# Two Q/K buffers, even projections, later Q/K copies and bank-by-bank score waits in an attention block

## The reference, cut to what matters

```
h  = layernorm(x);  a = rmsnorm(h) * ln1_w
q, k, v = a @ Wq.T, a @ Wk.T, a @ Wv.T          # 16 heads of 32 columns each
s = q @ k.T / sqrt(32), causal mask             # per head, 512 x 512
p = softmax(s)
mod = 0.1 * tanh((p @ v) @ Wo.T @ A)            # A: 512 x 16
gate = silu(h2 @ W_in.T + (mod * (h2 @ A)) @ B)
out = x + tanh(g) * ((gate * (h2 @ W_up.T)) @ W_down.T)
```

## Time and profile before

| | before |
|---|---|
| median of 3 runs | 1078.74 us (1078.07 to 1079.66) |
| the profiled execution | 1080.39 us, of which the span of the profile 1078.7 us |
| PE busy | 1035.0 us (96%), weight loads 860.9 us (80%) |
| DVE busy | 735.5 us (68%) |
| ACT busy | 613.1 us (57%) |
| POOL busy | 177.7 us (16%) |
| mean granted clock of PE | 0.997 |

### The profile page before, as it was taken

One profiled execution on the slowest core, in us unless ns is written; L12 is line 12 of the kernel. 1 busy time (PEld: TensorE's weight loads), 2 busy tenths in 40 slices (PEclk: granted clock), 3 DMA queues, 4 the chain that ended last, 5 costly groups with the idle time before them and its releaser, 6 DMA issues.

```text
span 1078.7 us, 17949 instructions
## 1 busy us (share of the span) xinstructions
PE 1035.0 (96%) x5336; PEld 860.9 (80%) x5337; DVE 735.5 (68%) x1662; ACT 613.1 (57%) x1463; POOL 177.7 (16%) x156
## 2 busy tenths in 40 slices
PE   6999999999999999989999999999999999899998
PEld 6787878777888888878888888778888877788887
DVE  7766747996665559985664589966655689854443
ACT  4464547886444458875444378864354588754342
POOL 4536122320000003320000024200000133200000
PEclk9899999999999999999999999999999999999999
DMA  6534132443322425243322354432234342333221
GB/s 244 188 141 165 39 118 70 97 100 120 105 88 90 151 69 140 64 119 128 108 89 88 108 142 97 112 117 88 88 102 141 85 121 68 79 91 105 88 88 49
DMA packets 47063, 115.59 MB, mean 107 GB/s; under 512 B 6800, under 2 KB 6800, under 8 KB 46096
## 3 DMA queue, kind: packets, MB, share of 16 engines
q1 hardware_dynamic: 43968, 105.06, 33.1%
q0 software_dynamic: 3040, 9.96, 2.7%
HBM read 76.46 MB, written 13.37 MB: 83 GB/s over the span
## 4 chain that ended last, share of the span: by engine, by line
PE 80%; DVE 9%; issue 3%; DMA 3%; ACT 2%; SPq 1%; POOL 1%; DVEq 0%; ACTq 0%; POOLq 0%
PE bank L510 64%; PE bank L709 4%; PE bank L722 3%; DVE wr L1326 3%; DVE nb L1338 3%; PE bank L681 3%; DMA stack<-wr 2%; PE bank L758 1%; SPq L307 1%; DVE big L1347 1%; PE bank L685 1%; ACT big L962 1%; PE bank L769 1%; PE bank L566 1%; DMA big<-in_x,gidx 1%
## 5 line engine op out<-in xcount | busy, mean ns | idle before, releaser
L510 PE MATMUL bank<-hT,wr 128*128 128x512 f32 x1488 | 358.4, 390 | 0.0
L510 PEld LDWEIGHTS bank<-hT,wr 128*128 128x128 f32 x1488 | 278.9, 188 | 59.9 <-issue 1.3
L510 PE MATMUL bank<-wr,actr 128*128 128x512 f32 (+1 forms) x1224 | 303.3, 397 | 2.2 <-DVE actr L1308 1.5
L510 PEld LDWEIGHTS bank<-wr,actr 128*128 128x128 f32 x1224 | 229.1, 190 | 51.1 <-issue 3.3
L1376 DVE SCALAR_TENSOR_TENSOR wr<-stream,lns,wr 128x256 fp32r<-128x256 f32 x256 | 122.3, 538 | 51.0 <-ACT wr L1001 51.0
L1326 DVE TENSOR_TENSOR wr<-bank,wr 128x512 fp32r<-128x512 f32 (+1 forms) x224 | 124.6, 600 | 19.7 <-ACT wr L878 19.7
L962 ACT ACTIVATE big<-bank,nb 128x512 f32<-128x512 f32 (+3 forms) x256 | 131.7, 531 | 9.7 <-DVE nb L1338 8.2
L878 ACT ACTIVATE actr<-act_sb 128x512 fp32r<-128x512 f32 x64 | 40.4, 632 | 145.7 <-DVE act_sb L1390 145.7
L878 ACT ACTIVATE wr<-bank 128x512 fp32r<-128x512 f32 (+1 forms) x224 | 102.6, 532 | 27.8 <-PE bank L510 18.7
L1013 ACT ACTIVATE sil<-bank 128x512 f32<-128x512 f32 x64 | 38.1, 596 | 137.6 <-PE bank L758 137.6
L485 POOL TENSOR_SCALAR big<-big,rr 128x256 f32<-128x256 f32 x64 | 78.0, 1219 | 205.9 <-DVE rr L1343 205.9
(11 more groups left out here) (182 smaller groups left out, 1078.6 us busy)
## 6 DMA issues: line engine op xcount, KB each, us to landing
stream<-in_wmlp SPq DMA_DIRECT2D x64, 512.0 KB, 4.0
stack<-wr SPq DMA_DIRECT2D x192, 128.0 KB, 2.3
stream<-in_wmlp SPq DMA_DIRECT2D x64, 256.0 KB, 2.7
big<-in_x SPq DMA_DIRECT2D x4, 1024.0 KB, 5.5
big<-y_rows SPq DMA_DIRECT2D x4, 1024.0 KB, 5.6
residual<-big SPq DMA_DIRECT2D x4, 1024.0 KB, 5.1
big<-residual SPq DMA_DIRECT2D x4, 1024.0 KB, 5.6
out<-big SPq DMA_DIRECT2D x3, 1024.0 KB, 4.5
```

What stands on the lines that cost most here:

```text
L510: mm = pe.matmul(dst, lhs(pl, k), rhs(pr, k), start=start and i == 0, stop=stop and i == n - 1, skip_group_check=skip)
```

## The change

There are two `qk` buffers, one for even and one for odd groups. The copies of Q and K from bank 3 (ACT's high part and DVE's low part) move to the end of a head's step, behind the copies of the turned probabilities, and to other heads: K of group q + 1 at j = 0, Q of group q + 2 at j = 2. PE's projections are cut in halves of 6 matmuls, one per head: j = 0 the second half of K of group q + 1, j = 1 and 2 the two halves of Q of group q + 2, j = 3 the first half of its K; the first half of K of group 1 comes ahead of head 0. The up product is spread in pairs of matmuls over heads 9 to 14. `scores` waits three times, for the first, third and fourth exponential, each ahead of the bank that they read. Normalising: DVE 512 and 256 columns, POOL 128 and 384, ACT none. POOL takes over the high part of the weights of groups 2 and 3, in halves of 512 columns. K of group 0 uses bank 3 instead of 7, and the second half of the values bank 6 instead of 7. The loops over q are written out.

```diff
-NORM_DVE, NORM_ACT, NORM_POOL = (3, 2), (0,), (1,)
+NORM_DVE, NORM_POOL = (3, 1), (0, 2)
-FIRST_QK = (6, 7)
-VALUES, LOW_RANK = (4, 7), 5
+FIRST_QK = (6, 3)
+VALUES, LOW_RANK = (4, 6), 5
+UP_PARTS = 6
+UP_FROM = H - 1 - UP_PARTS
...
-        qk = carve(6144, 2048).rearrange("p (m t) -> p m t", m=4)
+        qk = carve(6144, 4096).rearrange("p (n m t) -> p n m t", n=2, m=4)
...
             # POOL
             for b in range(NB):
-                weights_low(b, 1)
+                for which in range(2):
+                    weights_low(b, 1, which)
                 normalise(b * H)
                 for q in range(NQ):
                     for j in range(QH):
                         if q < NQ - 1 or j < QH - 1:
                             normalise((b * NQ + q) * QH + j + 1)
-                        if j == 1 and q < NQ - 2:
-                            weights_low(b, q + 2)
+                        if j < 2 and q < NQ - 2:
+                            weights_high(b, q + 2, j)
+                            weights_low(b, q + 2, j)
...
             # PE, scores
-                if not first:
-                    pe.wait_ge(exp_ok, n * 4)
+                if not first:
+                    pe.wait_ge(exp_ok, n * 4 - 3)
                 rows(3, True)
                 mask(0, 3 * P, 1)
+                if not first:
+                    pe.wait_ge(exp_ok, n * 4 - 1)
                 rows(2, True)
                 rows(0, False)
                 mask(1, 2 * P, 2)
+                if not first:
+                    pe.wait_ge(exp_ok, n * 4)
                 rows(1, True)
                 mask(2, P, 1)
...
             # PE, head_step
-                if j == 2 and ahead == 2:
-                    project(b, q + 2, 0, half=0)
-                if j == 0 and ahead:
-                    project(b, q + 1, 1)
-                if j == 3 and ahead == 2:
-                    project(b, q + 2, 0, half=1)
+                if j == 0 and q < NQ - 1:
+                    project(b, q + 1, 1, half=1)
+                elif j and q < NQ - 2:
+                    project(b, q + 2, (0, 0, 1)[j - 1], half=(0, 1, 0)[j - 1])
...
             # ACT, split_qk and head_step
-                if which == 0 and not first:
+                if which == 0 and q >= 2:
                     for k in range(2):
-                        act.wait_ge(stk[k], n * 96)
+                        act.wait_ge(stk[k], (n - 1) * 96)
...
-                    exponentials(n + 1, (j + 1) % 2)
-                    normalise(n + 1, (j + 1) % 2)
-                if j < 2 and ahead:
-                    split_qk(b, q + 1, j)
+                    exponentials(n + 1, (j + 1) % 2)
                 for i, (bk, w, at) in enumerate(((4, 512, 0), (5, 512, 512), (6, 256, 1024))):
                     act.wait_ge(p_turned, n * 3 + i + 1)
                     copy(pts[:, j % 2, HI, at:at + w], bank[bk][:, 0:w]).then_inc(pt_hi, 1)
                 if j == 0:
                     act.wait_ge(pv_done, b + 1 + n)
                     ...
+                if j == 0 and q < NQ - 1:
+                    split_qk(b, q + 1, 1)
+                elif j == 2 and q < NQ - 2:
+                    split_qk(b, q + 2, 0)
...
             # DVE, head_step
-                if j < 2 and ahead:
-                    qk_low(b, q + 1, j)
                 if two_more:
                     maxima(n + 2)
...
+                if j == 0 and q < NQ - 1:
+                    qk_low(b, q + 1, 1)
+                elif j == 2 and q < NQ - 2:
+                    qk_low(b, q + 2, 0)
```

More of the change, by code:

```diff
@@ L350, in batch @@
                     load_residual(b)
-                with sp.Fori(1, NQ) as q:
+                for q in range(1, NQ):
                     for j in range(QH):
@@ L468, in _ @@
                 if i == ITEMS - 4:
[L469 to L479, removed]
+                    for which in range(2):
+                        weights_low(0, 0, which)
             def normalise(n):
@@ L706, in turn_probs @@
                         pe.wait_ge(pt_lo, (n - 1) * 3 + (1, 2, 3)[kt])
+                    elif first and kt == 2:
+                        pe.wait_ge(vpb_ok, values_out)
                     for qt in range(kt, TT):
@@ L763, in up_product, with up_part @@
                               lambda p, k: hT[:, p, k, :], DT).then_inc(u_done, 1)
[L765 to L772, removed]
+            def up_part(par, part):
+                n = DT * len(PARTS) // UP_PARTS
+                for i in range(part * n, part * n + n):
+                    k, (pl, pr) = i // len(PARTS), PARTS[i % len(PARTS)]
+                    mm = pe.matmul(bank[UP[par]][:, :], wch[:, par, pl, (DT + k) * P:(DT + k) * P + P],
+                                   hT[:, pr, k, :], start=i == 0, stop=i == DT * len(PARTS) - 1,
+                                   skip_group_check=True)
+                if part == UP_PARTS - 1:
                     mm.then_inc(u_done, 1)
@@ L814, in batch @@
                 values((0, 1))
+                pe.matmul(bank[ATT][:, :], zeror[:, :], hT[:, HI, 0, :], start=True, stop=False,
+                          skip_group_check=True).then_inc(pv_done, 1)
                 pe.wait_ge(qk_lo, b * (NQ * 2) + 2)
@@ L823, in batch @@
                 pe.wait_ge(ha_ok, b + 1)
-                turn_probs(b * H, 0, first=True)
+                turn_probs(b * H, 0, first=True, values_out=b + 1)
                 scores(b * H + 2, 0, b * (H // 2) * 48 + 96)
[L827 to L830, removed]
+                project(b, 1, 1, half=0)
+                for q in range(NQ):
                     for j in range(QH):
-                        head_step(b, q, j, 2)
-                for q, ahead in ((NQ - 2, 1), (NQ - 1, 0)):
-                    for j in range(QH):
-                        head_step(b, q, j, ahead)
+                        head_step(b, q, j)
                 pe.wait_ge(exp_ok, (b + 1) * H * 4)
@@ L1329, in qk_low @@
                 dve.wait_ge(qk_hi, (b * NQ + q) * 2 + which + 1)
-                low(qk[:, (Q_LO, K_LO)[which], :], bank[at][:, :], qk[:, (Q_HI, K_HI)[which], :], qk_lo)
+                low(qk[:, q % 2, (Q_LO, K_LO)[which], :], bank[at][:, :], qk[:, q % 2, (Q_HI, K_HI)[which], :], qk_lo)
             def maxima(n):
```

101 lines of the change are left out of this document (47 added, 54 removed).

## The result

The changed kernel takes 1107.51 us (median of 4 runs, 1106.56 to 1108.15); the kernel before took 1079.20 beside it (4 runs, 1078.07 to 1080.14). The ratio is 1.0262, 95% interval 1.0244 to 1.028: slower by 28.3 us, where 19.9 were forecast. The profiled execution took 1107.2 with a span of 1105.1, 26.4 more span than before, at a granted clock of 0.998.

What follows compares the result with a forecast made beforehand. It took PE's work, and DVE's row in steps without projections, as the bound. Late copies cost 6.06 a batch, the tail gives 0.89 back: 5.2 a batch, 19.9 in all, 1098.7 us; range 1086 to 1113.

Steps and rivals of the forecast that it cites:

- The loop over the late copies: Heads 0 to 8: ACT's Q/K copy awaits its own step's projection, delaying exponentials and next transposes; two heads 11.11, not 9.30.
- The tail: From the start of head 10's transposes to the attention's end: 25.39 us, before 26.28, so 0.89 back per batch.
- light steps: Steps without a projection, behind the start of head 10's transposes: bound by DVE, 4.27 - 0.13 each.
- Turn(14) to (15): From the start of head 14's transposes to head 15's: 3.17 - 0.13 = 3.04 us.
- turn(12) to (14): Start of head 12's transposes to head 14's, through ACT's value copy that waits for attend of head 11: 9.94 us.
- turn(15) to the end: From the start of head 15's transposes: DVE's last low part 2.91 behind, plus attend 1.17 and 0.05: 4.13 us.
- Written-out loops: Loops over q without jumps: 0, bounds -2 to +2 us over the run for register instructions saved and code fetched.
- The sum: Whole run: 5.2 us longer per batch, 20.7 for four, less 0.75 already lost in batch 3: 19.9 us slower.
- rival 3: Normalising: POOL holds DVE's 256-column operation on the same tile, 0.5 longer in 9 places a batch, 1117 us; chance 0.12.
- rival 1: ACT's Q/K copies find their projections done: no stall, heads cost 4.65, 4.2 a batch gained, 1061 us; chance 0.12.
- rival 2: Each of five late Q/K copies delays a batch by less than 1.8; 0.8 would mean no change; chance 0.05.
- The wait by bank: Scores waiting for exponentials bank by bank on PE: gives 0.4 per late Q/K copy, nothing at heads without one.

Runs made afterwards that it cites:

- Experiment 1: Changed kernel with the Q and K copies moved one head on, ahead of the copies of the turned probabilities: 1078.47 us (ratio 1.0001).
- Experiment 4: Kernel before, with only ACT's and DVE's copy of K moved to the end of step j = 0: 1104.08 us (ratio 1.0249).
- Experiment 12: Changed kernel with values copied in halves and up matmuls behind attend, Q/K copies still at a step's end: 1098.50 us (ratio 1.0186).
- Experiment 2: Changed kernel with Q/K copies one step later and, in heads 9 to 14, up matmuls behind the scores: 1077.29 us (ratio 0.9987).
- Experiment 7: Kernel before, with only the new normalising split (DVE 512 + 256 columns, POOL 128 + 384, ACT none): 1077.23 us (ratio 0.9986).
- Experiment 5: Kernel before, with PE's loop over the first two groups of four heads written out: 1081.79 us (ratio 1.0025).
- Experiment 9: Changed kernel with Q/K copies one step later, values in halves, up matmuls behind attend, PE's first two groups looped again: 1059.04 us (ratio 0.981).
- experiment 3: Changed kernel with one wait of the scores for all four exponentials in place of three by bank: 1120.43 us (ratio 1.0391).
- Experiment 6: Kernel before, with only the scores' wait for exponentials made bank by bank: 1079.26 us (ratio 1.0003).
- Experiment 10: Changed kernel with Q/K copies one step later, values in halves, up matmuls behind attend, one scores wait: 1063.50 us (ratio 0.9857).

## Why the prediction was right, and where its size was off

The measured 1107.5 lies in the stated range, 1.5 above the 1090 to 1106 that the forecast's own mechanism had. The mechanism is the one forecast; the terms that were too small stand below.

**The loop over the late copies: right, term by term.** Copy 0.19 behind the projection's end (0.20); to the exponentials 0.50 (0.49); exponentials to reciprocal 421.94 to 424.11 = 2.17 (2.20); reciprocal to turn 424.11 to 427.43 = 3.32 (3.35); turn(2) to (3) 4.88 (4.87). Two heads 11.06 (11.11), though pairs with Q's copy at (3) to (4) take 11.20, since that copy began 0.33 behind its projection. Turn(1) to (9) 44.53 (44.44), turn(9) to (10) 6.18 (6.24). PE's idle time came to 9.4 a batch, not 11. Experiments 1, 4 and 12 show that the place of the copy is the cause, from three sides.

**The tail: mis-sized, 1.34 a batch.** From turn(10), 471.96, to the MLP's first matmul, 498.69, it takes 26.73, where I had 25.39 and before 26.28. Three steps of it:
- Two light steps from turn(10) to (12) take 4.61 and 4.60, not 4.14: together 0.93. I put them at DVE's row and didn't ask where the up matmuls stood. They are ahead of the scores, so 0.54 of them ends in DVE's wait for its maxima. Experiment 2, which moves them, shows 4.44 and 4.15: the second falls to my value, the first only by 0.17.
- Turn(14) to (15) takes 3.46, not 3.04. Before, that step had no wait and its 3.17 were PE's own work, so DVE's 0.13 had no place in it. The prediction said that POOL would be the bound where DVE has neither maxima nor low part to cover it, and then did not apply that at the last head, where the maxima are missing. POOL took 2.17, not 1.9. Experiment 7 shows the same step in the kernel before.
- The rest is right within 0.1: turn(12) to (14) 9.87 (9.94), turn(15) to the end 4.19 (4.13).

**Written-out loops: priced at 0, bounds -2 to +2, measured 3.** The edit is outside my bounds. Experiments 5 and 9 show it from both sides, +3.1 and -3.1.

**The sum.** 19.9 + 4 x 1.34 + 3 = 28.3, less what went better: turn(0) to (1) takes 5.02 in place of 5.57, 0.55 gained where I had 0.3, and turn(0) of batch 0 comes 0.6 earlier. That makes 26.7, against 26.4 in the spans and 28.3 between the medians; most of the 1.9 between these two is the profiled run before, which stands 1.2 above its median (1080.39 against 1079.20). I also read the idle times of turn(10) to (13) as 0.59 to 0.70; turn(11) has 0.55, which no term used.

**POOL and DVE on one tile (rival 3): fell.** Reciprocal to turn took 3.32, where rival 3 needed 0.5 more than 3.35. The pair of DVE operations got shorter, 0.86 (was 1.04), with POOL working from 424.38 to 426.55 across it. The second still seems slowed, since its 256 columns take 463 ns, nearly as long as the 512 ahead of it (487), but not held until POOL is done. The rule of the Trainium skill, SBUF — State Buffer, "SBUF: two separate sides", that one engine has the port pair for a whole instruction, would give rival 3's time, if POOL gets its turn between DVE's two. The page says it of DVE operations in a two-port mode or with two SBUF inputs, and no run here shows the mode of these. The trace speaks against that order, by 0.14 us: DVE's pair ends at 425.19, POOL's 128 columns (424.38 + 0.95, the mean of the group) at 425.33. Whether POOL is the one that waits, for both of DVE's, these rows leave open. Experiment 7 shows that the split alone isn't slower.

**No stall (rival 1) and in between (rival 2): fell.** ACT's waits of 2.91, 3.05 and 1.46 + 1.04 are longer than my 2.3. But rival 1's number was reached by another kernel: it gave 1061 when copies find their projection done. Moving them was not enough (1078.47); the second wait on ACT, which the late ones had hidden, had to go too (1062.09, with 3 us of jumps in it that rival 1 did not have, so the nearness is in part luck).

**The wait by bank: right in size, for another reason.** I gave it 0.4 per late copy, since PE's own work would end at P + 6.6 and not 6.24. By experiment 3 the single wait costs 12.9 us for 20 late copies, 0.65 each, but at full clock only 0.1: the turn behind it no longer waits and runs 0.22 shorter, which I left out (the step after takes 4.65, not 4.87). The rest comes with the granted clock, which I did not price. Experiments 6 and 10 give about nothing without late copies. The edit softened a stall that the same change made.

## What to carry to other kernels

In a queue that runs in order, a copy must stand behind the moment at which its input is ready, not only ahead of the moment at which its output is needed: look for what stands behind it (here the exponentials that the next turn hangs on) and give it one step's slack. When such a wait is taken away, look at once for the next one on the same engine: the kernel fell well under the one before (1079) only with both gone and the up matmuls moved (1107.5, 1078.5, 1062.1 us). When a wait grows, look at the clock of the steps behind it before you put the whole loss down to the wait. And when POOL takes over work that DVE covered, look at the last iteration, where the cover is missing.

## What the runs showed of the hardware that I had not expected

- A loop body that grows cost time at the jump back here: with PE's body longer by one written-out loop, the 24 matmuls behind the jump take 6.62 us (620.39 to 627.01) and not 5.44, with gaps of 0.25 and 0.88 in which PE waits for nothing that the profile shows; straight into the last batch there is none. I read it as fetching code; shown are the gaps, their place, and 3 us for two jumps.
- POOL's time hardly follows the columns: 948 ns for 128, 1219 for 256, 1239 for 384, where the 128 and the 256 run beside DVE's pair and the 384 mostly behind it.
- The granted clock fell to 0.79 over a step in six of the sixteen steps of experiment 3, behind waits of PE of 1.63 to 1.72 us ahead of the scores, and each such step took about 1.55 us more than its like at full clock (8.08 against 6.52, 8.17 against 6.62). In the changed kernel, where the same wait is split (0.26 to 0.40 and 0.35), no attention step shows it.
- A releaser's name can be the wrong one: a DMA for a projection (432.64), DVE's low part for POOL's end (494.50).
